# First attention's V projected token by token and moved to key rows through HBM, in place of 128 transposes on the tensor engine

## What is computed

```python
xq = jnp.einsum('bsh,oh->bso', x, wq)          # (8, 128, 1024)
xk = jnp.einsum('bsh,oh->bso', x, wk)
xv = jnp.einsum('bsh,oh->bso', x, wv)
xq = xq.reshape(bsz, N_HEADS, seqlen, HEAD_DIM) # token 8n+t, columns 64c..64c+63 -> head n, row 16t+c
xk = xk.reshape(bsz, N_HEADS, seqlen, HEAD_DIM)
xv = xv.reshape(bsz, N_HEADS, seqlen, HEAD_DIM)
scores = jnp.einsum('bhid,bhjd->bhij', xq, xk) * SCALE
scores = jax.nn.softmax(scores, axis=-1)
out = jnp.einsum('bhij,bhjd->bhid', scores, xv)
out = out.reshape(bsz, seqlen, N_HEADS * HEAD_DIM)
return jnp.einsum('bso,ho->bsh', out, wo)
```

## Time and profile before

| | us |
|---|---|
| median of three timed runs | 373.02 (372.59 to 373.35) |
| profiled execution, first to last instruction | 371.0 |
| the timed median less that span (launch and end) | 2.0 |
| PE busy / DVE busy / ACT busy | 274.2 / 250.2 / 170.9 |

### The profile page before, as it was taken

How to read it: one execution, slowest core, us unless ns; L and a number is a source line. 1 busy time by engine, 2 the same in 40 slices (tenths; PEclk the granted TensorE clock), 3 DMA queues, 4 the chain that set the end, 5 groups by cost and what they waited for, 6 DMA issues and landing times.

```text
span 371.0 us, 6872 instructions
## 1 busy us (share of the span) xinstructions
PE 274.2 (74%) x2578; PEld 222.8 (60%) x2578; DVE 250.2 (67%) x694; ACT 170.9 (46%) x338; POOL 62.9 (17%) x137
## 2 busy tenths in 40 slices
PE   0957678988999989979866697987868874650440
PEld 0946668987899889979755364655545542330120
DVE  4974895589667987586777674657625566767574
ACT  5973663676357944714422343353323352412543
POOL 8700000000003103045150128003300300000300
PEclk9988999999999999989998699898989996975555
DMA  7941023000400050000420043000300000000001
GB/s 264 353 106 31 2 43 72 2 0 16 101 2 0 4 114 2 2 2 29 79 22 2 11 77 42 2 3 7 69 14 0 3 2 0 0 0 1 2 0 57
DMA packets 11568, 14.21 MB, mean 38 GB/s; under 512 B 1552, under 2 KB 9360, under 8 KB 11024
## 3 DMA queue, kind: packets, MB, share of 16 engines
q1 hardware_dynamic: 11536, 13.78, 15.7%
HBM read 8.01 MB, written 1.57 MB: 26 GB/s over the span
## 4 chain that ended last, share of the span: by engine, by line
PE 37%; DVE 34%; DMA 11%; ACT 10%; issue 6%; SPq 2%; ACTq 0%; DVEq 0%
DVE arena L1082 9%; PE PS L562 4%; DMA arena<-arena 4%; PE PS L522 4%; PE PS L588 3%; DMA q_piece<-VN 3%; DVE OT L1124 3%; ACT arena L877 3%; PE PS L485 2%; ACT xt L910 2%; DVE w0l L1071 2%; PE PS L668 2%; DMA arena<-q_piece 2%; DVE stats L1145 2%; PE PS L535 1%
## 5 line engine op out<-in xcount | busy, mean ns | idle before, releaser
L1082 DVE TENSOR_TENSOR arena<-PS,arena 64x512 f16<-64x512 f32 x64 | 44.0, 688 | 4.4 <-ACT arena L877 3.2
L504 PE MATMUL PS<-xh,w0l 128*128 128x256 f32 x96 | 31.5, 328 | 16.7 <-ACT w0h L861 9.3
L877 ACT ACTIVATE arena<-PS 64x512 f16<-64x512 f32 x64 | 37.9, 592 | 12.7 <-PE PS L506 12.0
L963 ACT ACTIVATE PT<-PS 128x512 f32<-128x512 f32 x32 | 19.1, 597 | 45.7 <-PE PS L674 45.7
L405 POOL TENSOR_SCALAR shift<-mv 128x3 f32<-128x3 f32 (+1 forms) x6 | 1.4, 232 | 206.9 <-DVE mv L1148 206.9
L562 PE MATMUL PS<-V,PT 128*128 128x96 f32 x256 | 33.9, 276 | 2.5 <-DVE On L1111 2.5
L562 PEld LDWEIGHTS PS<-V,PT 128*128 128x128 f32 x256 | 31.8, 194 | 3.0 <-ACT PT L897 2.8
L890 ACT ACTIVATE V<-PS 64x256 f32<-64x256 f32 x64 | 24.0, 375 | 19.3 <-PE PS L522 18.6
L504 PEld LDWEIGHTS PS<-xh,w0l 128*128 128x128 f32 x96 | 19.0, 198 | 19.8 <-ACT w0h L861 9.3
L1234 DVE TENSOR_REDUCE rowmax<-PS 128x4 f32<-128x512 f32 x32 | 21.8, 685 | 13.4 <-PE PS L676 13.3
L910 ACT ACTIVATE xt<-res,shift,rstd 128x128 f32<-128x128 f32 x42 | 17.7, 483 | 24.7 <-DVE shift L1161 24.7
(11 more groups left out here) (214 smaller groups left out, 702.6 us busy)
## 6 DMA issues: line engine op xcount, KB each, us to landing
arena<-arena SPq DMA_DIRECT2D x8, 512.0 KB, 4.1
arena<-k_piece SPq DMA_DIRECT2D x8, 96.0 KB
arena<-q_piece SPq DMA_DIRECT2D x8, 96.0 KB
xT<-x_T SPq DMA_DIRECT2D x1, 512.0 KB, 3.7
w<-wk SPq DMA_DIRECT2D x2, 256.0 KB, 4.5
w<-wq SPq DMA_DIRECT2D x2, 256.0 KB, 6.0
w<-wv SPq DMA_DIRECT2D x2, 256.0 KB, 6.3
wo<-wo SPq DMA_DIRECT2D x1, 512.0 KB, 7.0
```

The costliest lines, as they stand in the source:

```text
L504: mm(dst, w0l[:, w, g], xh[:, x], start=True, stop=False)
L877: m = fn(dst[:, a], src[a * 64:(a + 1) * 64], ACT.Copy)
L1082: m = tt(lower[:, a], src[a * 64:(a + 1) * 64], upper[:, a], ALU.subtract)
```

## The change

V is projected with the tokens as the stationary operand and all of its 1024 output columns moving, 512 at a time, so a unit is 3 matmuls of 512 columns and its result has tokens on partitions. ACT copies a unit into `VN` contiguously. SP stores each sequence's 128 x 1024 floats to a tensor in HBM, where they lie in the order head, key row, 64 columns, and loads them back with the key rows on partitions, in pieces of 64 floats (256 bytes). `turn_v`, line 522, and its copies, line 890, are gone; a pair has 12 units and not 20, and V's four stand alone in ticks 3 to 6. Since V's rows now come in plain key order, K's columns must too: `by_column` writes K (units 0 to 3, high and low part) in the order (t, a, g), so that consecutive elements of one instruction are 16 float16 elements, 32 bytes, apart. Q is written as before. A number of semaphores were merged or renumbered; that changes no order.

```diff
-            v = buf.rearrange("p (n a g t) -> p a g n t", a=2, g=G, t=8)
+            if i < 4:
+                v = buf.rearrange("p (n t a g) -> p a g n t", a=2, g=G, t=8)
+            else:
+                v = buf.rearrange("p (n a g t) -> p a g n t", a=2, g=G, t=8)
...
-        PJ = ((0, 1, 2), (3, 4, 5), (6, 7), (8, 9), (10, 11), (12, 13), (14, 15, 16), (17, 18, 19))
+        PJ = ((0, 1, 2), (3, 4, 5), (6, 7), (8,), (9,), (10,), (11,), ())
...
         def v_there(p, q):
-            return (pj_free[q % 2], 10 * (p - 1) + (NPROJ + q) // 2 + 1) if p else (s("v_in"), q + 1)
+            return s(f"v_load{p % 2}{q // 4}"), 16 * (p // 2 + 1)
+
+        def projected_at(p, i):
+            if p:
+                return i % 2
+            return i if i < 8 else i - 4
+
+        def v_half(h):
+            return VN[:, h * 1024:(h + 1) * 1024]
...
                     sp.dma_start(dst[b][64:P, :], dst[b][0:64, :]).then_inc(qk_in[b], 16)
+                for h in range(2):
+                    sp.wait_ge(*((pj_free[1], 6 * (p - 1) + 5 + h) if p else (s("vn_in"), 2 * h + 2)))
+                    sp.dma_start(v_piece[2 * p + h].rearrange("n (t c) d -> (n t) (c d)", t=8), v_half(h))\
+                        .then_inc(s(f"v_out{h}"), 16)
+                for h in range(2):
+                    sp.wait_ge(s(f"v_out{h}"), 16 * (p + 1))
+                    if p >= 2:
+                        sp.wait_ge(s("pv_done"), QP * (p - 1))
+                    sp.dma_start(V[:, b, h * H:(h + 1) * H, 0:DH0], v_piece[2 * p + h].rearrange("n p d -> p n d"))\
+                        .then_inc(s(f"v_load{b}{h}"), 16)
...
+                if i >= 8:
+                    h, cols = (i - 8) // 2, slice((i % 2) * 512, (i % 2) * 512 + 512)
+                    x = slice(p * TP + h * P, p * TP + (h + 1) * P)
+                    mm(bank(at), xh[:, x], w0l[:, 2, cols], start=True, stop=False)
+                    mm(bank(at), xl[:, x], w0h[:, 2, cols], start=False, stop=False)
+                    mm(bank(at), xh[:, x], w0h[:, 2, cols], start=False, stop=True).then_inc(s("proj_done"), 1)
+                    return
...
-            for q in range(4):
-                turn_v(0, q)
-            pe.wait_ge(s("vn_in"), 4)
             for Q in range(AHEAD):
                 scores_q(Q)
-                if Q < 4:
-                    turn_v(0, 4 + Q)
...
-                    fn(by_head(VN[:], i), src, ACT.Copy).then_inc(s("vn_in") if p == 0 else pj_free[i % 2], 1)
+                    h = (i - 8) // 2
+                    if p and i % 2 == 0:
+                        act.wait_ge(s(f"v_out{h}"), 16 * p)
+                    fn(v_half(h)[:, (i % 2) * 512:(i % 2) * 512 + 512], bank(at), ACT.Copy)\
+                        .then_inc(s("vn_in") if p == 0 else pj_free[i % 2], 1)
```

More of the change, by code:

```diff
@@ L59, in decoder @@
     q_piece = nc.dram_tensor("q_piece", [2, P, NTOK], F16, kind="Internal").ap()
+    v_piece = nc.dram_tensor("v_piece", [NB, H, P, DH0], F32, kind="Internal").ap()
     with ExitStack() as ctx:
@@ L314, in _ @@
                 b = p % 2
-                lower = (pj_free[1], 10 * (p - 1) + 4) if p else (s("qk_lo"), 8)
+                lower = (pj_free[1], 6 * (p - 1) + 4) if p else (s("qk_lo"), 8)
                 for (split, count), dst in (((s("qk_hi"), 8 * p + 8), QA), (lower, QB)):
@@ L506, in project @@
                     m = mm(dst, w0h[:, w, g], xh[:, x], start=False, stop=True)
[L507 to L523, removed]
                 m.then_inc(s("proj_done"), 1)
@@ L560, in weigh @@
                     pe.wait_ge(s("norm_done"), Q)
+                else:
+                    pe.wait_ge(s("v_ones"), 1)
                 for h in range(4):
@@ L570, in turn_max @@
                 else:
-                    pe.wait_ge(s("v_in"), 8)
+                    pe.wait_ge(s("vn_in"), 4)
                 pe.wait_ge(s("max_done"), 4 * b + 4)
@@ L592, in project_next @@
                 for p, i in next_projection(t, k):
[L593 to L596, removed]
+                    project(p, i)
             def turn_x(g, k, at):
@@ L739, in late @@
                         pe.wait_ge(s("turn_free"), 8 * NPAIR)
-                        pe.wait_ge(s("qp_lo2"), 1)
-                        pe.wait_ge(s("ve_done2"), 1)
+                        pe.wait_ge(s("qp_lo"), 3)
+                        pe.wait_ge(s("ve_done"), 3)
                     else:
@@ L948, in mid @@
                     act.wait_ge(s("pe_k1a"), g + 1)
-                    fn(tokens(kph, g), part_of(bank(7), g), ACT.Identity, bias=b1[:, 1:2]).then_inc(s(f"kp_hi{g}"), 1)
+                    if g == 0:
+                        act.wait_ge(s("v_out0"), 16 * NPAIR)
+                        act.wait_ge(s("v_out1"), 16 * NPAIR)
+                    fn(tokens(kph, g), part_of(bank(7), g), ACT.Identity, bias=b1[:, 1:2]).then_inc(s("kp_hi"), 1)
                 if i == 20:
                     act.wait_ge(s("pe_q1a"), g + 1)
-                    fn(tokens(qph, g), part_of(bank(6), g), ACT.Identity, bias=b1[:, 0:1]).then_inc(s(f"qp_hi{g}"), 1)
+                    fn(tokens(qph, g), part_of(bank(6), g), ACT.Identity, bias=b1[:, 0:1]).then_inc(s("qp_hi"), 1)
             def scores(u):
@@ L1021, in _ @@
                 empty_projection(0, i)
-            act.wait_ge(s("v_ones"), 1)
-            for q in range(QP):
-                empty_turned_v(0, q)
             for t in range(TICKS0):
@@ L1075, in lower_parts @@
             def lower_parts(p, i):
-                at = i % 8 if p == 0 else i % 2
-                src = bank(at).rearrange("p (g n t) -> p g n t", g=2, t=8)
+                src = bank(projected_at(p, i)).rearrange("p (g n t) -> p g n t", g=2, t=8)
                 dve.wait_ge(s("qk_hi"), 8 * p + i + 1)
```

51 lines of the change are left out of this document (23 added, 28 removed).

## The result

The changed kernel takes 437.66 us (median of 4, 435.01 to 441.24) against 373.19 for the one before (median of 4, three of which gave the 373.02 known beforehand): ratio 1.1721, 95% interval 1.1657 to 1.1785. The forecast was 379.0 in a range of 363 to 388; slower was the side with the larger chance, but the time lies 50 us above the range.

The account below looks back on a forecast made before the run. Neither PE nor DVE was taken to bound the whole: DVE bounds the low-part stretches, PE those after the half copies. 373.0 less 10.0 for PE work removed, plus 16.0 for stepped K writes, gave 379.0 us, range 363 to 388.

Parts of the forecast that it names:

- the price of the step: K's stepped float16 writes in the DVE stretches: 0.5 us more per instruction, upper bound 0.82, 16 us in all.
- That all 32 of them count: All 32 DVE instructions on K lie in the four DVE stretches, so each microsecond on them is 32 on the end.
- ACT nothing, with 3 us if the hand-over shows: ACT's 32 K copies may slow but fit in the stretch: nothing, or 3 us if the hand-over to DVE shows.
- The gain of 10.0: PE work removed: 9.1 us in the stretches plus 1.6 at the start, less 0.7 for stretches not closing up.
- the rival called the clock: PE's clock may fall after longer idleness before the first scores: about 1.7 us per fall, 381; no separate chance.
- The transfers: V's stores 4.1 us and loads 6 us each, both covered; next pair's half copies lose nothing to SP's waits.
- The sum: Whole kernel: 373.0 less 10.0 gain plus 16.0 for K's steps, 379.0 us.
- the signs to look for: K halves 1.2 us, DVE stretches 4 longer and over 90% busy, PE stretches 2.8 shorter without gaps, first maxima 1.6 closer.
- steps that are free: Rival: DVE writes K at 0.69 us as before, only the gain is left, 363 to 367 us; chance 32%.
- a late V: Rival: at 13 us a load V comes late, +8 us, 387 with the step's price, 371 without; chance 4%.
- PE's time lost in the loop of normalising: Rival: weighing, normalising and output copies bind once transposes go, half the gain lost, 384 us; chance 6%.

Follow-up runs that it names:

- the twos: Changed kernel, same K layout, but ACT and DVE walk K with two neighbouring head groups innermost: 367.2 us, ratio 0.9804; run again, 369.17 us.
- the probe: Separate program timing single DVE and ACT instructions, 64 x 512 elements, PSUM source: lone float16 writes 2.29 to 2.41 us, lone float32 1.00 to 1.07.
- the run with only DVE stepped: Changed kernel with K's high part in runs (ACT's write, DVE's read), only DVE's write of the low part stepped: 419.65 us, ratio 1.1222.
- the step alone: Kernel before with only the stepped write and read of K's float16 parts added, V keeping its transposes: 441.6 us, ratio 1.1844.
- the one turned by GpSimd: Against the kernel before: K stays in runs, GpSimd reorders x's tokens for V, which is projected token-major, stored and loaded: 377.16 us, ratio 1.0078.

## Why the prediction was wrong

**The step that failed is the price of the step:** "0.5 us", with 0.82 as the upper bound from the earlier trace rows. It measures 2.30 - 0.69 = 1.61 us on DVE, twice the upper bound. The rows behind the bound are not stepped writes at all. They are `V_.reciprocal(rec[:, b % 2, :], o[:, :, DH1])` in line 1246 and its like in line 1110: the steps of 32 and 96 floats are in the read of PSUM, and the float32 result is written contiguously. A stepped read of PSUM is what the twos show to be free on DVE (689 against 688 ns), so whatever made sixteen elements dearer than four there, the slope says nothing of a stepped write. That a lone float32 write falls inside the bracket is luck: the probe gives 1.00 to 1.07 us against 0.68, 0.32 to 0.39 more. The estimate from the Trainium skill, "Vector Engine (DVE) Microarchitecture Reference", section on measured stream behaviour on trn2, 0.34 to 0.74 more, has its lower end where these float32 writes are. Neither speaks of a lone 2-byte write, and the text said so and went on to use 0.82 as a bound for it. A slope read from another element size and another side of the instruction is not a bound.

**That all 32 of them count** was right: 51.6 us measured for 32 x 1.61 with DVE alone.

**"ACT nothing, with 3 us if the hand-over shows"** was wrong: 18 us are measured. ACT's copies were given no price of their own, though the text named them; they take 2.32 us, as DVE's. What is added, by the starts of the half copies against the run with only DVE stepped (38.45, 80.38, 133.91, 185.66 there; 40.17, 85.55, 142.68, 201.77 in the changed kernel), is 1.7 at the start and 3.5, 3.6 and 7.3 in the next three spans. It shows as waiting of DVE: for ACT it is 19.8 us in all in the changed kernel and 5.2 with only DVE stepped, by the groups above. The likely reason for two of the spans is that DVE waits for ACT's first unit, whose two copies end 2 x 1.7 = 3.4 us later; this is argued from the sizes alone. The larger last one was not taken apart.

**The gain of 10.0** was too large as well: it measures 4.7 to 7.1. With the span of the first run in twos, 365.3 against 371.0: from the first half copy to pair 1's second, 27.50 us against 28.67, gain 1.2 (1.6 expected). From there to pair 2's, 39.24 against 39.93: 0.7 instead of 2.8. From there to the maximum after pair 3's PE stretch (158.94 and 152.34), 4.9 instead of 6.3. After it 0.9 is lost. The marks that are not in the earlier trace rows are, in the chain of the kernel before:

```profile
94.18 4.06 DMA arena<-arena
...
158.94 0.69 DVE rowmax L1087
```

And in the chain of the kernel in twos:

```profile
25.69 4.60 DMA arena<-arena
...
53.19 5.21 DMA arena<-arena
...
92.43 4.07 DMA arena<-arena
...
152.34 0.69 DVE rowmax L1084
```

Of the 2.1 us that pair 1 lacks the larger part is the rival called the clock. With unit 9 gone from tick 3, PE idles for 1.94 us where 2.1 were foreseen, and its next matmuls take 0.31 us each for the 0.22 to 0.23 that such a one takes at the upper level, in the twos' time order of PE:

```profile
58.45 0.29 PE L553 MATMUL PS<-arena 128*128 128x128 f16 x1 [1.94 <-DMA arena<-arena]
58.53 0.31 PE L554 MATMUL PS<-arena 128*128 128x128 f16 x1
```

A granted clock of 0.91 over 18.70 us is 1.7 us lost, as much as the forecast named for one such fall and left out of its sum; with unit 9 back in tick 3 the clock is back too. At the start 0.4 us are missing, and pair 0's half copy alone is 0.54 longer, 4.60 for 4.06. The rest of the shortfall, 0.4 us for pair 1, 1.4 later on (half of that had been taken off as 0.7) and the 0.9 after pair 3, was not taken apart.

**The transfers** were right: 4.9 us a load for 6 taken; V never late; the next pair's half copies unhindered (5.21 and 5.13 us for pairs 1 and 2 in the changed kernel, 5.20 and 5.03 with the step alone and no V transfers). One thing was missed: pair 0's half copy takes 4.6 us where 4.06 stood, with V's store issued right behind it. The store is what slows it: the copy takes 4.06 with the step alone and no stores (42.69 to 46.75), and 4.55 to 4.60 in eight profiled kernels with V's new route, with the step and without (4.38 in the one turned by GpSimd).

**The sum with the measured terms:** 373.2 - 6 + 51.5 + 18 = 436.7, against 437.66. It is a weak test: 18 is itself the changed kernel's time less that of the run with only DVE stepped. The term with a price of its own is 32 x 1.61 = 51.5.

**Of the signs to look for,** K's and Q's halves did part (2.30 and 0.69), but DVE was busy over 90% only in the first two of its four stretches (93, 92, 85 and 84%), and these grew by 14 to 18 us (the earlier trace rows against the windows above), not 4. The PE stretches had no gaps but were shorter by 0.1 and 0.2 us only. The five first maxima lie 3.64 us apart from first to last for 4.75, 1.1 closer for the 1.6 forecast. Of the rivals, steps that are free and a late V are refuted, and so is PE's time lost in the loop of normalising where the windows show PE without a gap, 18.66 of 18.70 us in the twos. Slower was forecast and slower came, with a chance of 0.59 given to it; the size was missed by the two prices.

## What to carry to other kernels

Before an element-wise instruction is given a strided output, look at the bytes that it writes in one piece and the distance to the next, not at the number of elements: lone float16 values 16 bytes or more apart cost more than three times a contiguous write, on both engines; 4 bytes apart they cost little, and two of them side by side cost nothing on DVE and 0.05 us on ACT. A bound for such a write has to come from a write, of the same element size: check which side of an instruction a step is on before taking a price from its row. The same layout in memory can be written either way, by which dimension of the access pattern is innermost; where an edit moves data between layouts, try the order of the walk before giving the layout up. And an engine whose copies another one reads must be priced with it: here ACT's slower copies added 18 us, though by busy time they seemed to fit.

## What the hardware showed that was not expected

- A write of 64 x 512 float16 takes 0.68 us contiguous, 0.72 with 4 bytes from one to the next, 1.28 with 8, 2.41 with 16, 2.29 with 32 and 2.37 with 64; float32 0.68 with 8, 1.05 with 16, 1.07 with 32, 1.00 with 64. ACT: 0.59, 0.73, 1.30, 2.42, 2.30, 2.38 and 0.61, 1.08, 1.06, 1.02. Why a lone float16 costs over twice a lone float32 is open.
- A stepped float16 input costs DVE 0.37 us when the output is contiguous (1.06), and none when the output is stepped too (2.29 both ways).
- Reading PSUM with a step of 256 floats, as the twos do, costs DVE nothing (689 against 688 ns).
- A load of 512 KB in 2048 pieces of 256 bytes to 128 partitions landed in 4.9 us (median of 8), where four loads of 512 pieces in all, each to 8 partitions, took 6.84.
- A store of 512 KB issued while a half copy is under way makes that copy 0.5 us longer: 4.6 for 4.06 us, and 5.69 for 5.21.
